# Graph layers on one core: finishing of a pair in layer 0 over three groups, and 64 rows a round gathered by ScalarE

## The reference

```python
# layer 0, with out_deg clipped at 1
t1 = x @ W1
msg = (t1[src] + (x[src] * x[dst]) @ W2) / (sqrt(out_deg[src]) * sqrt(out_deg[dst]))
agg = segment_sum(msg, dst)
e = leaky_relu(where(in_cnt > 0, t1 + agg, 0) + b0, 0.01)
e = e / maximum(norm(e), 1e-12)
x = layernorm(x + e)
# layer 1
xt = x @ W.T + b1
out = segment_sum(xt[src], dst) / (deg + 1)
result = layernorm(x + out)
```

## Time and profile before

| | us |
|---|---|
| median of three runs | 3845.7 |
| profiled execution, its own time | 3845.26 |
| its span | 3843.5 |
| POOL busy in the span | 2894.7 (75%), 3055 instructions |
| PE busy | 2707.4 (70%) |
| DVE busy | 1930.4 (50%) |
| ACT busy | 497.7 (13%) |

### The profile page before, as it was taken

One profiled execution on the slowest core, in us unless ns is written; L12 is line 12 of the kernel. 1 busy time (PEld: TensorE's weight loads), 2 busy tenths in 40 slices (PEclk: granted clock), 3 DMA queues, 4 the chain that ended last, 5 costly groups with the idle time before them and its releaser, 6 DMA issues.

```text
span 3843.5 us, 66285 instructions
## 1 busy us (share of the span) xinstructions
PE 2707.4 (70%) x10342; PEld 1851.4 (48%) x10342; DVE 1930.4 (50%) x3848; ACT 497.7 (13%) x1540; POOL 2894.7 (75%) x3055
## 2 busy tenths in 40 slices
PE   4552777777767666667777777777777777777776
PEld 3442556555555555656644443434444444344443
DVE  8996566666666566666642333333333333333333
ACT  8992000000000000000000000000000000000000
POOL 7777777777777777777777777777777777777776
PEclk5555888888888888888877777877787877777777
DMA  7879455555555555555444444444444444444443
GB/s 254 274 237 337 151 164 166 163 165 164 164 164 165 164 164 164 165 164 163 146 125 122 129 126 129 125 131 124 132 125 130 125 127 127 129 127 130 126 127 113
DMA packets 327431, 598.55 MB, mean 156 GB/s; under 512 B 72589, under 2 KB 211394, under 8 KB 327074
## 3 DMA queue, kind: packets, MB, share of 16 engines
q0 software_dynamic: 145680, 398.00, 36.4%
q1 hardware_dynamic: 153528, 174.96, 13.8%
q10 hardware_dynamic: 27866, 22.52, 1.9%
HBM read 507.24 MB, written 76.03 MB: 152 GB/s over the span
## 4 chain that ended last, share of the span: by engine, by line
POOL 32%; SPq 23%; issue 22%; ACTq 9%; DMA 6%; ACT 5%; PE 2%; DVE 1%; DVEq 0%; POOLq 0%
POOL ring L709 32%; SPq L517 16%; ACT dst_rel L797 4%; ACTq L907 4%; SPq L510 4%; DMA ring<-x,idx 3%; PE banks L1603 2%; ACTq L818 1%; ACTq L932 1%; ACTq L884 1%; DMA ring<-src_lo 1%; DMA src_lo<-scaled_x 1%; SPq L438 1%; SPq L433 1%; SPq L491 1%
## 5 line engine op out<-in xcount | busy, mean ns | idle before, releaser
L1603 PE MATMUL banks<-ring,hot_space 128*128 128x257 f32 x6252 | 2095.9, 472 | 567.3 <-DMA ring<-x,idx 464.8
L1603 PEld LDWEIGHTS banks<-ring,hot_space 128*128 128x128 f32 x6252 | 1274.8, 226 | 1319.3 <-DMA ring<-x,idx 946.5
L709 POOL DMA_INDIRECT ring<-x,idx x1506 | 1426.7, 947 | 461.9 <-issue 451.9
L709 POOL DMA_INDIRECT ring<-scaled_x,idx x1241 | 1188.7, 958 | 381.0 <-issue 372.1
L1272 DVE SCALAR_TENSOR_TENSOR big<-banks,here_mask,big 128x257 f32 x784 | 343.2, 479 | 1342.9 <-PE banks L1603 1328.1
L1174 DVE TENSOR_TENSOR hot_space<-banks,dst_rel 128x1024 f32<-128x1024 f32 x344 | 421.0, 1225 | 175.7 <-issue 174.2
L1534 PE MATMUL banks<-ident,halves 128*128 128x128 f32 x588 | 136.2, 392 | 370.3 <-DVE halves L1286 368.5
L720 POOL DMA_INDIRECT ring<-in_x,src_col x276 | 263.9, 956 | 84.3 <-issue 83.8
L1534 PEld LDWEIGHTS banks<-ident,halves 128*128 128x128 f32 x588 | 105.3, 204 | 408.4 <-DVE halves L1286 363.7
L797 ACT ACTIVATE dst_rel<-columns,halves 128x128 bf16<-128x128 f32 x960 | 268.3, 377 | 5.3 <-DVE halves L1087 5.3
L836 ACT COPY idx<-src_col 128x32 int32 (+1 forms) x97 | 21.1, 218 | 1827.9 <-issue 915.0
(11 more groups left out here) (149 smaller groups left out, 1241.2 us busy)
## 6 DMA issues: line engine op xcount, KB each, us to landing
src_lo<-x ACTq DMA_DIRECT2D x3648, 1.0 KB
src_lo<-x SPq DMA_DIRECT2D x3648, 1.0 KB
src_lo<-scaled_x SPq DMA_DIRECT2D x2944, 1.0 KB
kept_rows<-ring SPq DMA_DIRECT2D x94, 384.0 KB, 3.2
ring<-kept_rows SPq DMA_DIRECT2D x47, 768.0 KB
ring<-x,idx POOLq DMA_INDIRECT x1506
src_lo<-scaled_x ACTq DMA_DIRECT2D x1408, 1.0 KB
ring<-scaled_x,idx POOLq DMA_INDIRECT x1241
```

Of the source, the lines that this page charges most:

```text
L709: g.indirect_dma_start(ring[:, u, 0:D], None, rows, bass.IndirectOffsetOnAxis(ap=idx[:, idx_buf(layer, n), u:u + 1], axis=0)).then_inc(row ...
L1603: last = nc.tensor.matmul(group_sum(k % SUMS), dst_hot[:, k % HOTS, u - k * GT, :], ring[:, u, 0:DW], start=u == tiles[0], stop=u == tiles ...
```

## The change

It has three parts, all in layer 0 except where said.

1. **x in two buffers.** `x_t` becomes two pairs of buffers, one for even and one for odd pairs (both layers). SP loads the rows of pair i in round i between its two blocks of 32 rows, and for that waits for the moments of pair i-2, no longer for those of pair i-1. It stores pair i-2 at the round's end, no longer pair i-1. In layer 1 the load stays at the round's end, with the shorter wait.
2. **Finishing over three groups.** DVE does `finish_sums` after the first group, `mix` of the next pair and then `moments` after the second, `norm` after the third. The last round is as before.
3. **ACT gathers 64 rows a round** (`first_round`, in place of `round_`), in five blocks of 16, 16, 8, 12 and 12 around its other work, for the last tile of all odd rounds 3, 5, ..., 47. POOL no longer gathers the last tile of rounds 3, 7, ..., 47: 12 gathers fewer. The rows' first block stands behind `next_idx`.

`base_row` and `base_row_f` move into `out_t` to make room. DVE's loop over rounds has two rounds in its body, for the two buffers.

The diff, cut to its core:

```diff
-FEW = SPANS
-ACT_BLOCKS = (((0, 16), None, None, (16, 32)), ((0, 24), (24, 32), (32, 48), (48, 64)))
+ACT_BLOCKS = (((0, 16), (16, 32), (32, 40), (40, 52), (52, 64)), ((0, 24), (24, 32), (32, 48), (48, 64)))
...
-        x_t = [sb(f"x_t{n}", [P, D]) for n in range(2)]
+        x_space = sb("x_space", [P, 4, D])
+        x_t = [[x_space[:, 2 * n + s, :] for s in range(2)] for n in range(2)]
...
+            def next_x(layer, m, buf):
+
+                if layer or not (isinstance(m, int) and m == 0):
+                    sp.wait_ge(var_ready, node_no(layer, m))
+                for s in range(2):
+                    load_x(layer, m + 1, 2 * m + 2 + s, s, buf)
...
+                if layer == 0:
+                    next_x(layer, i - 1, buf)
+                if hand is not None:
                     hand_part(layer, hand, 2 * half + 1, load_next)
                 if extra is not None:
                     extra_part(*extra)
-                next_pair(layer, i - 1)
+                if layer == 1:
+                    next_x(layer, i - 1, buf)
+                    store_pair(layer, i - 1)
+                elif not (isinstance(i, int) and i == 1):
+                    store_pair(layer, i - 2)
...
                     for i in range(2, SPAN):
-                        gather_round(layer, i, i, HAND_U if layer or i % 2 == 0 else U, first)
+                        gather_round(layer, i, i, HAND_U, first)
                     with g.Fori(1, SPANS + 1) as h:
                         for n in range(SPAN):
                             gather_round(layer, SPAN * h + n, n,
-                                         (HAND_U, EXTRA_U)[n == SPAN - 1] if layer else (HAND_U, U)[n == SPAN - 1], first)
+                                         EXTRA_U if layer and n == SPAN - 1 else HAND_U, first)
...
+            def first_round(i, n, sums, ended, last=False, hand=None, share=0, passed=None):
+
+                first_row = share * 2 * HAND_ROWS
+                next_idx(0, i, n)
+                if passed is not None:
+                    pass_hand(0, passed)
+                if hand is not None:
+                    if share == 0:
+                        hand_loaded(0, hand)
+                    starts = load_starts(0, hand, share * 2, False)
+                    if share == 0:
+                        hand_free(0, hand)
+                    hand_block(0, first_row, 0, starts)
+                if ended:
+                    norm_root(i - 2)
+                if hand is not None:
+                    hand_block(0, first_row, 1, starts)
+                    starts = load_starts(0, hand, share * 2 + 1, share == 1 and not (isinstance(hand, int) and hand == HANDS))
+                    hand_block(0, first_row, 2, starts)
+                if sums and not last:
+                    clear_sums(i - 1)
+                if ended:
+                    var_root(0, i - 2)
+                if hand is not None:
+                    hand_block(0, first_row, 3, starts)
+                if sums:
+                    take_turned(0, i - 1)
+                if last:
+                    norm_root(i - 1)
+                if hand is not None:
+                    hand_block(0, first_row, 4, starts)
...
                     if ended and k == 0:
-                        finish_sums(layer, i - 2, acc[:, bass.ds(2 * i - 4, 2), :])
-                        moments(layer, i - 2)
-                    if ended and k == LAST_K and not last:
+                        finish_sums(layer, i - 2, acc[:, bass.ds(2 * i - 4, 2), :], x_arrived(layer, buf, turn - 1), x_t[buf])
+                        if whole:
+                            moments(layer, i - 2, x_t[buf])
+                    if ended and k == LAST_K and layer == 1 and not last:
                         norm(layer, i - 2)
                     if sums and k == LAST_K and layer == 0:
-                        mix(i - 1, acc[:, bass.ds(2 * i - 2, 2), :])
+                        mix(i - 1, acc[:, bass.ds(2 * i - 2, 2), :], x_arrived(0, 1 - buf, turn - 1 + buf), x_t[1 - buf])
+                        if ended and not last:
+                            moments(layer, i - 2, x_t[buf])
+                    if ended and k == LAST_K + 1 and not whole:
+                        norm(layer, i - 2)
                     if last and k == LAST_K:
                         norm(layer, i - 2)
-                        finish_sums(layer, i - 1, acc[:, NW - 4:NW - 2, :])
+                        finish_sums(layer, i - 1, acc[:, NW - 4:NW - 2, :], x_arrived(layer, 1, turn - 1), x_t[1])
```

More of the change, by code:

```diff
@@ L457, in next_x @@
                     load_x(layer, m + 1, 2 * m + 2 + s, s)
-            def store_pair(layer, m):
-                for s in range(2):
-                    store(layer, m, 2 * m + s, s)
-            def next_pair(layer, m, last=False):
-                if last:
-                    sp.wait_ge(var_ready, node_no(layer, m) + 1)
-                else:
-                    next_x(layer, m)
                 store_pair(layer, m)
@@ L610, in _ @@
                         middle_round(layer, 2, hand=2, half=0)
-                        middle_round(layer, 3, hand=2, half=1, load_next=True, extra=(1, 0))
+                        middle_round(layer, 3, hand=2, half=1, load_next=True, extra=(1, 0), buf=1)
                         pass_hand(layer, 2)
@@ L631, in _ @@
                         sp.sem_inc(table1_whole, 1)
-                    next_pair(layer, ROUNDS - 2, last=True)
+                    store_pair(layer, ENDS - 1)
                     if layer == 0:
@@ L943, in round_ @@
             def round_(layer, i, n, sums, ended, last=False, hand=None, share=0, passed=None, extra=None):
[L945 to L948 removed]
+                first_row = share * 2 * HAND_ROWS
+                load_next = share == 1 and not (isinstance(hand, int) and hand == HANDS)
                 if hand is not None:
@@ L951, in round_ @@
                         hand_loaded(layer, hand)
-                    starts = load_starts(layer, hand, share * parts, load_next and parts == 1)
+                    starts = load_starts(layer, hand, share * 2, False)
                 if passed is not None:
@@ L962, in round_ @@
                     roots(layer, i - 2)
-                if hand is not None and parts == 2:
+                if hand is not None:
                     hand_block(layer, first_row, 1, starts)
-                if sums and layer == 0 and not last:
-                    clear_sums(i - 1)
-                if sums and layer == 1:
+                if sums:
                     act.wait_ge(groups_added, group_no(layer, i, LAST_K + 1) + SUMS)
                     take_sums(i - 1, acc[:, bass.ds(2 * i - 2, 2), :])
-                if hand is not None and parts == 2:
-                    starts = load_starts(layer, hand, share * parts + 1, load_next)
+                if hand is not None:
+                    starts = load_starts(layer, hand, share * 2 + 1, load_next)
                     hand_block(layer, first_row, 2, starts)
@@ L974, in round_ @@
                     take_turned(layer, i - 1)
-                if last and layer == 0:
-                    norm_root(i - 1)
-                elif last:
+                if last:
                     var_root(layer, i - 1)
@@ new lines, in _ @@
+                        first_round(1, 1, True, False, hand=1)
+                        first_round(2, 0, True, True, hand=1, share=1)
+                        first_round(3, 1, True, True, hand=2, passed=1)
+                        with act.Fori(1, SPANS) as g:
+                            first_round(SPAN * g, 0, True, True, hand=2 * g, share=1)
+                            first_round(SPAN * g + 1, 1, True, True, hand=2 * g + 1, passed=2 * g)
+                            first_round(SPAN * g + 2, 0, True, True, hand=2 * g + 1, share=1)
+                            first_round(SPAN * g + 3, 1, True, True, hand=2 * g + 2, passed=2 * g + 1)
@@ new lines, in _ @@
+                        first_round(SPAN * SPANS, 0, True, True, hand=HANDS - 1, share=1)
+                        first_round(SPAN * SPANS + 1, 1, True, True, hand=HANDS, passed=HANDS - 1)
+                        first_round(SPAN * SPANS + 2, 0, True, True, hand=HANDS, share=1)
+                        first_round(SPAN * SPANS + 3, 1, True, True, passed=HANDS)
+                        first_round(ROUNDS - 1, ROUNDS - 1, True, True, last=True)
+                    else:
+                        round_(layer, 0, 0, False, False)
+                        round_(layer, 1, 1, True, False, hand=1)
@@ L1262, in _, with x_arrived @@
             nc.vector.memset(ring[:, :, D:DW], 1.0).then_inc(ring_ones, 1)
+            def x_arrived(layer, buf, turn):
+                return x_in[buf], x_count(layer, buf, turn)
             def load_block(i, k):
@@ L1274, in add_group, with mix @@
                 last.then_inc(groups_added, 1)
-            def mix(m, sums, xs=x_now, mask=pair[0], last=False):
```

(4 more changed lines are left out.)

141 lines of the change are left out of this document (68 added, 73 removed).

## The result

The changed kernel takes 3938.2 us (median of four runs, 3937.46 to 3941.05) against 3848.4 of the kernel before on the same chips: ratio 1.0238, interval 1.0226 to 1.0251. The forecast was 3830.5 with a range up to 3842, so it is wrong in sign and size.

What follows compares the result with a forecast made beforehand. POOL was taken as the bound, at 1.263 us a gather. 12 gathers fewer gave -15.2 us and the other three parts 0, from 3845.26 to 3830.1, with the median at 3830.5; 8-in-10 range down to 3827, up to 3842.

Steps and rivals of the forecast that it cites:

- A gather less is 1.263 us less, with no gap of POOL: POOL, layer 0: 12 gathers fewer at 1.263 us each give -15.2 us, as long as nothing makes POOL wait.
- SP issues as much as before, so its pair stays at 64.05: SP, layer 0: moving the x loads leaves a pair of rounds at 64.05 us against POOL's 63.2; value 0.
- never waits: SP in the kernel before: a shade slower than POOL at 64.05 us a pair, with no waits of its own.
- more rows in flight may land later: ACT's sequencer, layer 0: an argument for the rival that ACT becomes the bound; no size given.
- The start: SP, early layer 0: tile passed at about 442.5, SP 14.7 us earlier from there on, offsetting 19 us lost over 22 pairs.
- Finishing over three groups, 0: DVE: same instructions in another order; PE's 308.8 us wait for `mix` shrinks but is off the path; value 0.
- The room of PE, 18 us: PE against POOL's ring, layer 0: SP or ACT may be late by up to 18 us at no cost.
- ACT's pair, 63.4: ACT, layer 0: 64 rows a round take 63.4 us a pair, 65.1 at most; value 0, cost range 0 to 24.
- ACT becomes the bound: Rival: ACT's sequencer in layer 0 sets the pace from 64.7 us a pair; 3866 us at 65.6; chance 0.10.
- SP or ACT are late, but less: Rival, layer 0: a pair at 64.3 or SP's start partly lost, stall of 7 us, 3837.5 us; chance 0.12.
- ACT's hand-overs more than 64 us apart: Sign in layer 0 that, with POOL gaps growing in its second half, would point to ACT as the bound.
- the fixed 2.0 us: Skill page's fixed DMA cost; would make ACT's pair an estimated 60.9 us; the forecast used the trace's rows instead.

Runs made afterwards that it cites:

- e10: Changed kernel with 4 of each 32 rows that SP issues in layer 0 left out: 3834.1 us, ratio 0.9971.
- e16: Kernel before plus two x buffers and finishing over three groups, x loads at the round's end, ScalarE at 32 rows: 3847.9 us, ratio 1.0004.
- e1: Changed kernel with ScalarE back at 32 rows a round and POOL at its 12 gathers, x loads in mid-round: 3864.6 us, ratio 1.0043.
- e3: Changed kernel with SP's layer 0 loads of x back behind the second 32 rows, ahead of the stores: 3920.9 us.
- e11: Changed kernel with the second half of each of ScalarE's five layer 0 blocks left out, 32 rows instead of 64: 3844.1 us, ratio 0.9996.
- e17: Changed kernel with two buffers for SP's rows, later hand-over, two pairs per loop body, and x loads at the round's end: 3909.3 us.
- e4: Changed kernel with SP's hand-over moved behind its next load of kept rows and places: 3965.1 us.
- e14: Changed kernel with two buffers for SP's rows in layer 0, later hand-over, and two pairs per loop body: 3874.4 us, ratio 1.0081.
- e6: Changed kernel with SP's stores of a pair issued after 16 of the second 32 rows instead of behind them: 3924.6 us.
- e9: Changed kernel with each of ScalarE's layer 0 rows cut to its first 128 of 1024 bytes, as many DMAs: 3927.7 us.
- e5: Changed kernel with ScalarE's first 16 rows of every second round issued behind the root instead of ahead of it: 3985.0 us.

## Why the prediction was wrong, step by step

- **A gather less is 1.263 us less, with no gap of POOL.** Right as far as nothing makes POOL wait: e10 has the forecast's picture, 3834.1 us, POOL without gaps, and its last gather at 1925.27 where "near 1922" was said. In the changed kernel it isn't used.
- **"SP issues as much as before, so its pair stays at 64.05".** This step failed. The issues were counted and the waits were put at nothing ("never waits"), though SP's own waits before show 3.6 us in 6 times for its rows. In the kernel before, the tile was passed on 2.61 us after the last row, and that looked like issue; it was a landing wait just covered by two loads and two stores. Moving the loads uncovered 1.15 us of it and put a wait for the moments in their place (e16 to e1: 16.7 us; with 64 rows of ScalarE's, changed kernel to e3, 17.3, but there the wait for rows stays as it is). The dearer part is that the landing is no constant: it is 1.7 and 2.7 us with 32 of ScalarE's rows a round (e11, e1) and 6.0 with 64, and from e1 to the changed kernel the time grows by 73.6 us. Together the pair is 69.3. The forecast had "more rows in flight may land later", but for ScalarE's rows only; for SP's this term was put at nothing.
- **The start.** 444.55 against "about 442.5": right, and worth 18.2 us, as against 110.8 lost behind it.
- **Finishing over three groups, 0.** Right by itself at ScalarE's 32 rows (e16). Not seen was the new dependence: `finish_sums` comes sooner and needs the buffer that SP's stores free, so that PE's wait for `mix` stayed at 298 us where less was forecast.
- **The room of PE, 18 us.** SP's 69.3 lose 6.1 us a pair on POOL's 63.2, so that this room and the head start of 18 are gone after six pairs.
- **ACT's pair, 63.4.** In e10 ScalarE, at 64 rows, keeps up with a pair of 63.8. The rival "ACT becomes the bound" was not what happened, though in e17 ScalarE's copy is a part of what stands right behind. The forecast's sign for it, ACT's hand-overs more than 64 us apart, misleads: they are 69.25 apart in the changed kernel and 63.46 in e10, with as many rows of ScalarE, so ScalarE was held up there and not holding. The rival "SP or ACT are late, but less" had the right engine and a stall of 7 us where the measured time lies 108 above the forecast.
- **Of the Trainium skill** (DMA: Bandwidth & Descriptors, Anatomy of one DMA) the forecast set aside the fixed 2.0 us for the trace's 4.3 to 5.05 on ScalarE. That section gives its figure for DMAs issued from GpSimd, and the DMAs here are issued from ScalarE and SyncE. What was not asked is what the landing was on SP and what it depends on. Landings from 1.7 to 7.2 us for the same DMA on SP (e11, e3) say that no fixed figure serves here.

## What to carry to other kernels

An engine that "never waits" may have a wait covered to the last tenth: before a step is moved away from behind an issue, read the time from the last issue to what needs it, and ask for its cover. Ask also what another engine's DMAs do to it: from 32 to 64 rows of ScalarE's a round SP's wait for its own rows went from 1.3 us a pair to 4.3 (e1, the changed kernel). Where one buffer is filled, copied on and filled again, both landings are in the cycle, and moving the hand-over only traded one wait for the other (e4). And when a repair brings less than its theory promised, split the gain: with a second buffer and a loop of two pairs (e14) the waits fell by 0.9 us a pair and the rest by 2.5.

## What the runs showed of the hardware

- SP's rows of 1 KB land later the more DMAs ScalarE issues in the same rounds: 1.7 to 2.7 us at 32 rows a round (e11, e1), 4.8 to 7.2 at 64 (the changed kernel, e3, e6), and 5.7 with rows of 128 bytes (e9). So it goes by the number of DMAs, not by the bytes, with a DMA share of 0.53 in the changed kernel; and not by the number alone, since e11 and e1 have the same and differ by 1.0 us. A moment's overlap doesn't do it: in e1, at 16 of 17 hand-overs, ScalarE issues during 4.5 to 7.5 of the 10.7 us of SP's last 32 rows, and they land after 2.3 to 3.3 us (at the last it issues nothing, and they land after 1.1). Nor is it what ScalarE issues behind them: in e5, at five of 16 hand-overs, it issues nothing between the last row and the hand-over, and they take 4.7 to 7.4 us all the same. What in the chip queues up was not found.
- At 64 rows, DMAs that SP issues behind its rows cover nothing of the wait for them: 4.5 us a pair with none (e6), 4.3 with two (the changed kernel), 4.2 with four (e3).
- On ScalarE a load of starts or the index copy stands between the last row and the hand-over, so that time (4.2 to 5.4 us before, 5.3 on average in the changed kernel) can't be read as plainly.
- In e9's profiled execution the mean granted clock was 0.823, in the changed kernel's 0.776. It is no effect of the shorter rows: the other three executions of e9 had 0.776 to 0.779. The one with 0.823 was also the slowest of the four, 3930.05 us, so the clock did not set the time here.
